# A vision block on one core: linear attention with one difference per direction and sums in PSUM, paired half-row matmuls, split first loads and another order of steps

## The reference

```
af, bf, mf = scan(w, k, v)              # forward; the state is read before token t is added
ab, bb, mb = scan(w, k[::-1], v[::-1])  # the same, backward
step: mm = max(m + w, k); e1 = exp(m + w - mm); e2 = exp(k - mm)
      a = e1*a + e2*v;  b = e1*b + e2;  m = mm
M = max(mf, mb, k + u);  ef = exp(mf - M); eb = exp(mb - M); ec = exp(k + u - M)
y = (ef*af + eb*ab + ec*v) / (ef*bf + eb*bb + ec)
x = x + (sigmoid(r) * y) @ Wo.T
```

## Time and profile before

| what | value |
|---|---|
| median of 3 runs | 350.29 us (349.79 to 350.33) |
| the profiled execution | 347.99 us |
| its span | 345.8 us, 2.2 us less than its time |
| PE busy | 310.9 us, 90% |
| DVE busy | 196.3 us, 57% |
| ACT busy | 184.0 us, 53% |
| POOL busy | 83.5 us, 24% |
| mean granted clock | 0.962 |

### The profile page before, as it was taken

One profiled execution on the slowest core, in us unless ns is written; L12 is line 12 of the kernel. 1 busy time (PEld: TensorE's weight loads), 2 busy tenths in 40 slices (PEclk: granted clock), 3 DMA queues, 4 the chain that ended last, 5 costly groups with the idle time before them and its releaser, 6 DMA issues.

```text
span 345.8 us, 7256 instructions
## 1 busy us (share of the span) xinstructions
PE 310.9 (90%) x2477; PEld 266.9 (77%) x2477; DVE 196.3 (57%) x524; ACT 184.0 (53%) x488; POOL 83.5 (24%) x85
## 2 busy tenths in 40 slices
PE   8988996997788899999989799996999999999980
PEld 5976783775576699779868687886998989998880
DVE  1736998799987612245474886885243334433440
ACT  1054446945584556484797897133455444555440
POOL 9710002001000201000100000013156554566532
PEclk9999999899699989999998999999899999999996
DMA  8980000000000790100769624132033233323322
GB/s 263 366 261 0 1 2 1 0 0 2 0 0 2 254 291 28 42 2 23 201 207 265 182 84 154 48 106 61 18 56 41 46 54 56 54 41 55 58 29 25
DMA packets 23296, 29.20 MB, mean 84 GB/s; under 512 B 5962, under 2 KB 18746, under 8 KB 23258
## 3 DMA queue, kind: packets, MB, share of 16 engines
q1 hardware_dynamic: 19370, 23.89, 22.6%
q0 software_dynamic: 3888, 4.81, 8.7%
HBM read 23.58 MB, written 5.11 MB: 83 GB/s over the span
## 4 chain that ended last, share of the span: by engine, by line
PE 32%; DMA 23%; DVE 20%; issue 12%; ACT 8%; POOL 1%; DVEq 1%; POOLq 1%; SPq 1%; ACTq 0%
DMA out<-ffn 20%; PE banks L1358 7%; PE banks L1359 6%; PE banks L1461 4%; PE banks L1388 3%; PE banks L1518 2%; PE banks L1506 2%; DMA patch<-in_xp 2%; PE banks L1403 2%; DMA vs<-v_scratch 2%; DVE st L1009 2%; DVE arena L1083 1%; DVE arena L1089 1%; PE banks L1489 1%; POOL rs L672 1%
## 5 line engine op out<-in xcount | busy, mean ns | idle before, releaser
L672 POOL TENSOR_TENSOR rs<-va,consts 128x4 f32<-128x4 f32 (+3 forms) x16 | 15.4, 962 | 189.8 <-DVE va L1016 106.2
L704 POOL DMA_INDIRECT out<-ffn x20 | 32.3, 1614 | 43.9 <-DVE ffn L1315 34.8
L1609 PE MATMUL banks<-arena,ffn 128*128 x240 | 42.7, 328 | 0.0
L1609 PEld LDWEIGHTS banks<-arena,ffn 128*128 128x128 f32 x240 | 38.5, 190 | 0.5 <-issue 0.2
L941 ACT ACTIVATE ffn<-banks,chans 128x128 f32<-128x128 f32 x21 | 9.6, 457 | 48.3 <-PE banks L1582 48.3
L694 POOL DMA_INDIRECT vs<-xh_scratch,ffn x21 | 21.6, 1030 | 14.9 <-DVE ffn L1282 6.6
L1461 PE MATMUL banks<-rvw,ffn 128*128 128x192 f32 x108 | 20.4, 342 | 1.5 <-ACT ffn L851 1.5
L773 ACT ACTIVATE ht<-banks,chans 128x256 f32<-128x256 f32 (+3 forms) x32 | 16.7, 589 | 8.3 <-PE banks L1403 8.1
L1461 PEld LDWEIGHTS banks<-rvw,ffn 128*128 128x128 f32 x108 | 18.9, 201 | 2.0 <-ACT ffn L851 2.0
L1403 PE MATMUL banks<-consts,xh 128*128 128x128 f32 (+1 forms) x72 | 11.4, 286 | 9.1 <-ACT xh L757 7.1
L1388 PE MATMUL banks<-arena,patch 128*128 128x192 f32 x108 | 19.1, 330 | 0.1
(11 more groups left out here) (227 smaller groups left out, 747.3 us busy)
## 6 DMA issues: line engine op xcount, KB each, us to landing
arena<-in_w SPq DMA_DIRECT2D x8, 576.0 KB, 7.6
patch<-in_xp SPq DMA_DIRECT2D x9, 384.0 KB, 6.6
arena<-in_w1a SPq DMA_DIRECT2D x8, 384.0 KB, 6.9
vs<-v_scratch SPq DMA_DIRECT2D x24, 114.8 KB
arena<-in_w1b SPq DMA_DIRECT2D x16, 96.0 KB, 5.6
out<-h SPq DMA_DIRECT2D x1, 864.0 KB, 4.3
ffn<-in_kfw SPq DMA_DIRECT2D x1, 768.0 KB, 8.1
patch<-in_b SPq DMA_DIRECT2D x1, 768.0 KB, 4.5
```

The lines of the kernel that those rows point to most:

```text
L672: pool.tensor_tensor(RS[:, 0:n, sl], VA[:, 0:n, sl], power, ALU.pow).then_inc(rstd_ready, 1)
L704: pool.indirect_dma_start(out[:, :], bass.IndirectOffsetOnAxis(ap=IS[:, j:j + 1], axis=0), YG[j % 2], None, compute_op=ALU.add).then_inc(s ...
L1609: ins = mm(ps[:, 0:C], HST[j % 2][:, 128 * k:128 * (k + 1)], W2[:, bass.ds(e, 1), C * k:C * (k + 1)], start=(k == 0), stop=(k == HB - 1))
```

## The change

1. **One difference per direction.** `sub` is now two steps per batch: PE makes `d = m_before - k` only. Since m is the greater of `m_before + w` and `k`, `e2 = exp(-relu(d + w))` and `e1 = exp(-relu(-d - w))`. ACT takes three Relu of 288 elements from the banks and then one Exp of 864 in SBUF, for each of the four exponentials.
2. **Sums by PE.** The products of numerator and denominator stay on DVE (three each, of which `ec` is used as it is). PE adds them: `sum:c:0` and `sum:c:1`, three banks each, three identity matmuls a bank. ACT and DVE read the sums from PSUM, in thirds of 288 elements.
3. **Half-row pairs** in `kf` (now three steps of two blocks a batch) and in `qk` (q and k): the 128-row matmuls first, then two 64-row matmuls, one on rows 0 to 63, one on rows 64 to 127. For that ACT writes the 64-channel block of `HT` twice in the turns of kinds 2 and b, and memsets and one more load set the weight rows.
4. **First loads in thirds**: patch weight and tile 0 in three loads each.
5. **Another `ORDER`**, and `FILL` with 11 instead of 5 idle matmuls before the first expert transpose and 3 before the second.

```diff
-FILL = "kvr:0:0=4 kvr:0:1=3 logits:2=3 turn:g:3=5 logits:3=3 rank=6 list=14 xt:0=5"
+FILL = "kvr:0:0=4 kvr:0:1=3 logits:2=3 turn:g:3=5 logits:3=3 rank=6 list=14 xt:0=11 xt:1=3"
@@ ACT, wexp
-                            act.wait_ge(den_ready, c)
+                            act.wait_ge(z_ready, c)
-                            if what[1] == "1":
-                                ins = A(dst, src, ACT.Exp, bias=WU[:, i // 2:i // 2 + 1])
+                            ins = A(x[:, GI * i:GI * (i + 1), :], src, ACT.Relu, bias=WU[:, w:w + 1], scale=1.0 if first else -1.0)
...
+                        A(x, x, ACT.Exp, scale=-1.0).then_inc(exp_ready, 1)
@@ ACT, turn
+                        if b == 1 and step[1] in TWICE:
+                            ins = A(HT[C1:128, b, ...], ps[0:rows, ...], ACT.Identity, ...)
@@ DVE, wkv
                 if part == 5:
-                    ch.then(TTR(t1, p[0], before(EVF), ALU.mult))
-                    ch.step(TTR(t2, p[1], behind(EVB), ALU.mult))
-                    ch.step(TTR(t1, t1, t2, ALU.add))
-                    ch.step(TTR(t2, p[2], here(v), ALU.mult))
-                    ch.step(TTR(t1, t1, t2, ALU.add))
+                    TTR(here(E1F), p[0], before(E2F), ALU.mult).then_inc(product_ready, 1)
+                    TTR(here(E1B), p[1], behind(E2B), ALU.mult).then_inc(product_ready, 1)
                 if part == 6:
+                    TTR(t1, p[0], before(EVF), ALU.mult).then_inc(product_ready, 1)
+                    TTR(t2, p[1], behind(EVB), ALU.mult).then_inc(product_ready, 1)
+                    dve.wait_ge(product_ready, 5 * c + 3)
+                    TTR(p[0], p[2], here(v), ALU.mult).then_inc(product_ready, 1)
                 if part == 7:
+                    for i in range(3):   # numerator from PSUM, then denominator from PSUM
+                        freed(STT(here(EVF)[:, images, :], here(er)[:, images, :], 1.0, num, ALU.add, ALU.mult), ("sum", c, 1, i))
+                        freed(TTR(p[1][:, images, :], den, seed[:, images, :], ALU.mult), ("sum", c, 0, i))
@@ PE
+            def side_by_side(dst, moving, stationary, jobs):
+                for ps, st in zip(dst, stationary):
+                    mm(ps, st[0], moving[0], start=True, stop=False)
+                for i, (ps, st, job) in enumerate(zip(dst, stationary, jobs)):
+                    r = slice(C1 * i, C1 * (i + 1))
+                    end(mm(ps, st[1][r], moving[1][r], start=False, stop=True), job)
+                elif kind == "sum":
+                    pe.wait_ge(product_ready, 5 * c + (2, 5)[k])
...
+                        for n, x in enumerate(terms):
+                            ins = mm(ps, ident, x[:, images, :], start=(n == 0), stop=(n == 2))
```

More of the change, by code:

```diff
@@ L146 @@
-logits:0 vm:0:3 ot:10 pt:12 apply:g:1 pt:13 base:0 proj:2 stats:g:2 ot:11 turn:g:1 vm:1:3 pv:12 pv:13 pt:14 pt:15
-ot:12 ot:13 apply:g:2 pv:14 pv:15 turn:g:2 ot:14 ot:15 proj:3 stats:g:3 logits:1 logits:2 apply:g:3 base:1 base:2
-base:3 turn:g:3 logits:3
+tok:0 tok:1 tok:2 stats:a:0 apply:a:0 tok:3 tok:4 tok:5 stats:a:1 turn:a:0 kvr:0:0 apply:a:1 turn:a:1 kvr:0:1 wkv:0:0
+wkv:0:1 tok:6 tok:7 tok:8 stats:a:2 stats:a:3 kvr:1:0 kvr:1:1 apply:a:2 apply:a:3 sub:0:0 wexp:0:0 wkv:0:2 wexp:0:1
+wkv:0:3 sub:0:1 wexp:0:2 wexp:0:3 wexp:0:4 turn:a:2 turn:a:3 kvr:2:0 kvr:2:1 kvr:0:2 wexp:0:5 wkv:0:4 wkv:0:5 wkv:0:6
@@ new lines @@
+sum:0:0 sum:0:1 rc:0 kvr:0:3 kvr:1:3 wkv:0:7 wkv:1:0 wkv:1:1 wo:0 wo:1 wkv:1:2 sub:1:0 wexp:1:0 kvr:1:2 wexp:1:1
+stats:2:0 stats:2:1 sub:1:1 wexp:1:2 wexp:1:3 apply:2:0 wkv:1:3 apply:2:1 turn:2:0 wexp:1:4 wkv:1:4 wkv:1:5 kvr:2:2
+kf:0:0 hx:0 hx:1 kvr:2:3 wexp:1:5 sum:1:0 wkv:1:6 rc:1 sum:1:1 kf:1:0 kf:2:0 turn:2:1 wkv:1:7 wo:2 wo:3 hx:2 hx:3
+stats:2:2 stats:2:3 apply:2:2 apply:2:3 rv:0 rv:1 ff:0 kf:0:1 kf:1:1 kf:2:1 turn:2:2 stats:b:0 rv:2 rv:3 kf:0:2 ff:1
+kf:1:2 apply:b:0 turn:b:0 kf:2:2 turn:2:3 vt:0 stats:b:1 apply:b:1 turn:b:1 rv:4 rv:5 kf:0:3 ff:2 qk:0 spread:1:0
@@ L167 @@
 WARM = 4
+TWICE = "2b"
 ON_ACT = "a2 a3 20 21 22 23"
@@ L174, in kvr_blocks, with kf_blocks @@
     return range(1) if w == 1 else range(2)
-def kf_blocks(half):
-    return range(HB // 2 * half, HB // 2 * (half + 1))
+def kf_blocks(part):
+    return range(2 * part, 2 * part + 2)
 def jobs_of(step):
@@ L189, in jobs_of @@
         return [("sub", step[1], x, i) for i in range(3)]
+    if kind == "sum":
+        return [("sum", step[1], x, i) for i in range(3)]
     if kind == "kvr":
@@ L831, in _ @@
+                            if first:
+                                ch.then(ins)
+                            else:
+                                freed(ins, job)
+                        if first:
+                            ch.settle()
+                        else:
+                            for i in range(3):
+                                taken(act, ("sub", c, step[2] // 2, i))
+                        A(x, x, ACT.Exp, scale=-1.0).then_inc(exp_ready, 1)
                 if kind == "rc":
@@ L832, in _ @@
                     c = g
-                    den, seed = (dense(P3[:, WN * i:WN * (i + 1)]) for i in range(2))
+                    seed = here(E1F)
                     act.wait_ge(wu_ready, 1)
                     A(KB[:, NH:NH + 1], WU[:, 0:1], ACT.Abs_reciprocal_sqrt)
-                    act.wait_ge(den_ready, c + 1)
-                    ch.step(A(seed, den, ACT.Abs_reciprocal_sqrt))
+                    for i in range(3):
+                        src = full(act, ("sum", c, 0, i))[:, 0:GT].rearrange("p (i t) -> p i t", t=NT)
+                        ch.then(A(seed[:, GI * i:GI * (i + 1), :], src, ACT.Abs_reciprocal_sqrt))
@@ L1103, in wkv @@
                     dve.wait_ge(r_ready, c + 1)
-                    ch.step(STT(here(EVF), here(er), 1.0, t1, ALU.add, ALU.mult))
-                if part == 7:
+                    for i in range(3):
+                        images = slice(GI * i, GI * (i + 1))
+                        num = full(dve, ("sum", c, 1, i))[:, 0:GT].rearrange("p (i t) -> p i t", t=NT)
+                        freed(STT(here(EVF)[:, images, :], here(er)[:, images, :], 1.0, num, ALU.add, ALU.mult), ("sum", c, 1, i))
@@ L1107, in wkv @@
                     dve.wait_ge(seed_ready, c + 1)
-                    ch.step(TTR(p[2], p[0], p[1], ALU.mult))
-                    ch.step(STT(p[2], p[2], -2.0, p[1], ALU.add, ALU.mult))
+                    for i in range(3):
+                        images = slice(GI * i, GI * (i + 1))
+                        den = full(dve, ("sum", c, 0, i))[:, 0:GT].rearrange("p (i t) -> p i t", t=NT)
+                        freed(TTR(p[1][:, images, :], den, seed[:, images, :], ALU.mult), ("sum", c, 0, i))
@@ L1110, in wkv @@
+                    for k in range(2):
+                        for i in range(3):
+                            taken(dve, ("sum", c, k, i))
+                    ch.step(STT(p[2], p[1], -2.0, seed, ALU.add, ALU.mult))
                     STT(dense(Z[c]), p[2], -0.5, here(EVF), ALU.mult, ALU.mult).then_inc(z_ready, 1)
```

117 lines of the change are left out of this document (66 added, 51 removed).

## The result

The kernel after takes 355.12 us (353.76 to 356.89, 4 runs) against 350.31 us (349.79 to 351.20, 4 runs): a ratio of 1.0138 [1.0087, 1.0189]. I had said 346.2, with 340 to 353. So it is slower, by 4.8 us, and outside the range.

What follows compares the result with a forecast made beforehand. It took DVE's chain to bound the linear attention and PE's queue 108 to 200 us. Terms 0.2 + 1.0 - 1.4 - 1.9 - 0.7 - 1.6 + 0.3 = -4.1 us took the median from 350.29 to 346.2, range 340.0 to 353.0.

Steps and rivals of the forecast that it cites:

- After it: Attention behind the linear attention: kf and qk pairs give -1.4 us, shorter PE waits from the new order -1.9 us.
- one of the prediction's signs of being wrong: Attention: the prediction is wrong if the end of `rv:5` to the last `logits` gets longer than before.
- the term of the waits: Attention: of some 6 us of PE waits and half-speed loss, the new order saves a third, -1.9 us.
- First loads, +0.3: Start: four more issues delay tile 4 by up to 2.5 us, but little arrives; +0.3, between -0.3 and +2.5.
- Linear attention and feed-forward, +0.2: Up to the end of `rv:5`: last Z at 106.9, feed-forward no longer starves; +0.2 us, range -5 to +6.
- Half clock, +1.0: Linear attention: PE's waits before the sums and `turn:2:0` cost more half-speed work; +1.0 us, between 0 and 8.8.
- rival 1: Linear attention: sums run at half clock, 8.8 us a step instead of 4.4; 354.0 us in all, chance 0.18.
- Pairs, -1.4 here: Half-row pairs of the last batch's `kf` (0.9) and of `qk` (0.5), after the linear attention: -1.4 us.
- Rival 2: `kf` and `qk`: pairs gain what halving gives, 7.8 us instead of 2.1; 341 us in all, chance 0.10.
- each matmul removed counts nearly in full: From 108 to 200 us: PE's queue is the bound, busy 86.8 of 92.1 us, so removed matmuls save nearly their time.
- Last norm, -0.7: Last norm before the gate: DVE takes the power without standing behind two `logits` steps, as `apply:g:3` comes first; -0.7 us.
- Idle matmuls, -1.6: Expert stage start: more idle matmuls keep PE's clock up, 3.94 us become 2.3; -1.6 us, handed on through the scatters.

Runs made afterwards that it cites:

- e1_whole_loads: The changed kernel with the patch weight and tile 0 loaded whole again, in two issues instead of six: 352.6 us, ratio 1.0138 to the kernel before.
- f1_no_pairs: The changed kernel with kf and qk as 128-row products again and no second writes of HT: 355.4 us, ratio 1.0227 to the kernel before.
- f3_one_difference: The kernel before (old order, whole first loads, sums on DVE) plus one difference per direction, pairs and more idle matmuls: 346.6 us, ratio 1.0007.
- f4_before_fill: The kernel before with only the idle matmuls changed, 11 ahead of the first expert transpose and 3 ahead of the second: 348.46 us, ratio 1.0013.

## Why the prediction was wrong, step by step

The step that failed is "**After it** ... The new order moves `vt`, `qk` and the k spreads ahead. I give it a third, -1.9". With the pairs and the last norm it made -4.0 from the end of `rv:5` to the last `logits`; that this stretch gets longer was one of the prediction's signs of being wrong. Measured, without `qk:0` (2.9 us), which before stood ahead of that point: 81.1 us before (143.16 to 224.24), 86.55 - 2.93 = 83.6 after (144.20 to 230.75), so +2.5. I read the waits of PE alone. The steps `vl:1:g` also issue two experts' weights each on SP's queue, and I did not walk that queue. Eight of these loads stand ahead of the store of `vt:3` in both orders; before, v was stored long before it was needed, and the new order has `vt:3` just ahead of its use. "The new order moves `vt` ... ahead" is not so for this step: it came 12 us later. With the loads taken away the same stretch is 77.1 us (142.98 to 223.01, less 2.93), which is -4.0. The loads are 6.6 of the 9 us that were missed. That what is left agrees with the forecast to 0.1 us is in part luck, as no run shows the pairs' share of it. With the pairs and the norm as forecast the term of the waits came out at +4.6, beyond its bounds of -6 to +3.

The other terms:
- **First loads, +0.3, measured +1.4**: the upper part of the bounds (+2.5). I argued that the queues are still full; but tile 4 landed as much later as it was issued later, and `e1_whole_loads` undid it.
- **Linear attention and feed-forward, +0.2**: `rv:5` ends at 144.20, against 140.25 for before without `qk:0` (143.16 less 2.91), so +4.0, of which 1.4 is the start and 2.6 its own. The last Z came at 109.4, less the start 108.0, where I had 106.9. The Z path was 15.0 and not 14.4 us, since DVE's first read waits 3.4 us for the second sum. The prediction's own terms, 13.6 and the 1.2 by which the first sum delays the second, add up to 14.8; it took 14.4 without a reason. `rv:0` and `rv:1`, now behind that Z, were counted; that the feed-forward then saves 3.3 us of starving was true in part: its half clock went (1.00 instead of 0.95 over 35 us, some 1.7 us of work), but PE is still idle 1.3 us, where it was 1.6.
- **Half clock, +1.0**: before it was 1.5 + 3.6 us of work in the two batches ((1 - 0.96) x 38.6 and (1 - 0.91) x 40.1), after 0 + 3.5. So the loss fell by 1.6 us instead of rising. The sums did not fall into it, rival 1's mechanism is refuted, and the time near its 354.0 is a coincidence.
- **Pairs, -1.4 here**: each step measured near what was derived. A visit of two 256-column blocks takes 1.70 us (predicted 1.64, unpaired 1.73), of 384 columns 2.23 where unpaired it was 2.58, of 288 1.86 instead of 1.94. Rival 2 (1.3 us) is refuted. But no run shows this as time: `f1_no_pairs`, which undoes them, takes no more time from the last Z to the last `logits`, and `f3_one_difference`, which has the pairs in the order of before, takes 116.1 us there against 116.2. So "each matmul removed counts nearly in full" has nothing here to bear it out. That PE, busy 87 of 92 us, waits between, and that its waits took up the gain, would explain it and is not tested.
- **Last norm, -0.7**: DVE waits for POOL's power and takes it as it comes (226.23, after 0.96 us), where it took it 0.75 us late. As forecast.
- **Idle matmuls, -1.6**: 5.70 to 4.15 us and 11.30 to 9.73, as predicted. The total doesn't show it (`f4_before_fill`), as the chain of scatters varies by 4.6 us between traces.
- **The resolution**: the prediction took 0.7 us (0.2%) for what a measurement tells from no change. The intervals above reach 0.3% to 0.8% to either side.

With the measured terms the sum is 1.4 + 2.6 + 2.5 + 0.4 - 1.6 = +5.3, as in the traces up to the first scatter; the 0.4, from the last `logits` to the first transpose, was not forecast.
